# Another order of the stages on all four engines of a one-core transformer tower

## What is computed

```python
x = emb[tokens] * sqrt(D) + pe
scores = einsum('d,bijd->bij', attn_scale, tanh((x@Wq + bq)[:, :, None, :] + (x@Wk + bk)[:, None, :, :]))
h = layer_norm(x + softmax(scores) @ (x@Wv + bv) @ Wo + bo) ; h = layer_norm(h + relu(h@W1 + bf1)@W2 + bf2)
h = h + causal_attention_8_heads(ln(h))
t = ln(ln(h)) ; moe = the two best of 64 experts for every token ; shared = (silu(t@Ws1 + bs1)@Ws2 + bs2) * 0.25
out = h + ln(h) + (moe + shared) + silu(ln(moe + shared)@Wf1 + bf1)@Wf2 + bf2
```

## Time and profile before

| | us |
|---|---|
| median of three runs | 824.73 |
| the profiled execution | 828.12 |
| its span, first to last instruction | 826.1 |
| first `add` | 25.27 |
| end of the last `add` | 505.5 |
| count of all tokens (L1649) | 583.23 |

### The profile page before, as it was taken

The page is one execution under the profiler, slowest core; times in us unless marked ns, Lnnn a source line. Parts: engine busy times, 40 slices in busy tenths (PEclk is TensorE's granted clock), DMA queues, the critical chain, the costliest instruction groups (busy, mean ns, idle before and its releaser), DMA issues.

```text
span 826.1 us, 21375 instructions
## 1 busy us (share of the span) xinstructions
PE 742.8 (90%) x7238; PEld 600.6 (73%) x7238; DVE 622.6 (75%) x1635; ACT 623.8 (76%) x1471; POOL 353.2 (43%) x466
## 2 busy tenths in 40 slices
PE   0656799999999999999999999987789999999898
PEld 0533567777777677677677677765679999999787
DVE  0699999999999999999999996543423435443685
ACT  0477899999999999999999999764235556665354
POOL 3101223444644544554544543666126545555111
PEclk9988999999999999999999999998889999999999
DMA  3940000000000000000000000000299999994511
GB/s 82 261 93 6 7 2 7 14 13 12 18 14 11 16 16 12 16 16 11 16 16 12 11 16 7 16 15 25 88 342 393 376 394 401 320 359 160 160 32 38
DMA packets 50096, 78.99 MB, mean 96 GB/s; under 512 B 7428, under 2 KB 34203, under 8 KB 50000
## 3 DMA queue, kind: packets, MB, share of 16 engines
q1 hardware_dynamic: 33824, 65.01, 22.9%
q0 software_dynamic: 5664, 7.92, 3.5%
q10 hardware_dynamic: 10512, 4.83, 2.1%
HBM read 63.95 MB, written 15.92 MB: 97 GB/s over the span
## 4 chain that ended last, share of the span: by engine, by line
DVE 45%; PE 33%; issue 11%; POOL 3%; ACT 2%; SPq 2%; DMA 2%; ACTq 1%; POOLq 0%; DVEq 0%
DVE arena L939 27%; PE big L1693 9%; PE b_qk L1704 4%; PE b_s L1704 4%; DVE mx L1069 3%; PE big L1749 3%; SPq L404 2%; PE b_s L1762 2%; DVE stat_h L982 1%; PE b_qk L1762 1%; DVE stat_x L982 1%; POOL rows_dram L616 1%; PE big L1496 1%; PE b_s L1383 1%; PE b_t L1686 1%
## 5 line engine op out<-in xcount | busy, mean ns | idle before, releaser
L939 DVE TENSOR_TENSOR arena<-qT,b_qk 128x2304 f32<-128x2304 f32 x128 | 323.2, 2540 | 3.4 <-PE b_s L1383 3.2
L683 ACT ACTIVATE arena<-arena 128x2304 f32<-128x2304 f32 x128 | 272.4, 2133 | 10.3 <-DVE arena L939 10.2
L1383 PE MATMUL b_s<-arena,apad 128*32 128x192 f32 x3072 | 149.6, 333 | 4.2 <-ACT arena L683 3.5
L846 ACT ACTIVATE act_h<-big,arena 128x128 f32<-128x128 f32 x324 | 92.7, 369 | 71.9 <-PE big L1693 66.1
L1383 PEld LDWEIGHTS b_s<-arena,apad 128*32 128x32 f32 x3072 | 89.5, 111 | 48.3 <-issue 13.8
L651 POOL DMA_INDIRECT eo_dram<-gT,toff x81 | 79.8, 985 | 96.6 <-DVE gT L1268 92.9
L579 POOL TENSOR_TENSOR kept<-kept,rs 96x384 f32<-96x384 f32 x64 | 52.7, 824 | 120.7 <-DVE rs L1075 120.5
L1693 PE MATMUL big<-hbT,arena 128*128 128x128 f32 x648 | 87.2, 278 | 1.6 <-DVE hbT L1257 1.6
L747 ACT ACTIVATE kept<-big,mx 96x96 f32<-96x96 f32 x256 | 83.5, 350 | 2.6 <-DVE mx L1069 2.6
L1693 PEld LDWEIGHTS big<-hbT,arena 128*128 128x128 f32 x648 | 80.1, 194 | 2.0 <-issue 1.3
L616 POOL DMA_INDIRECT rows_dram<-rows_now,slots x64 | 61.4, 960 | 42.8 <-DVE slots L1123 30.2
(11 more groups left out here) (227 smaller groups left out, 1410.8 us busy)
## 6 DMA issues: line engine op xcount, KB each, us to landing
arena<-in_wpack SPq DMA_DIRECT2D x81, 578.0 KB, 10.0
prT<-rows_dram ACTq DMA_DIRECT2D x73, 64.5 KB
rows_dram<-act_h SPq DMA_DIRECT2D x1, 4128.0 KB, 23.4
arena<-eo_dram SPq DMA_DIRECT2D x4, 512.0 KB, 7.4
x_dram<-res SPq DMA_DIRECT2D x16, 96.0 KB, 1.7
out<-of SPq DMA_DIRECT2D x12, 128.0 KB, 1.8
eo_dram<-gT,toff POOLq DMA_INDIRECT x81, 5.6
rows_dram<-rows_now,slots POOLq DMA_INDIRECT x64, 2.3
```

The source lines that it names most:

```text
L683: act.activation(v, v, ACT.Tanh).then_inc(s["tanh"], 1)
L846: last = act.activation(act_h[:, i, c * TILE:(c + 1) * TILE], big[i][:, c * TILE:(c + 1) * TILE], ACT.Silu, bias=wslot[:, slot, 2 * DFF + ...
L939: dve.tensor_tensor(ring[c % TRING].rearrange("p (x m n) -> p x m n", m=CQ, n=N), qv.unsqueeze(3).to_broadcast([D, SPLIT * QG, CQ, N]), kv ...
L1383: last = pe.matmul(b_s[32 * a:32 * a + 32, 0:SPLIT * N], apad[:, 31 - line:63 - line], t[:, :, a, m, :], start=(line == 0), stop=(line == ...
```

## The change

No stage is added, removed or altered, and every stage runs as often as before. The four `body` lists and the three bank orders are written in another order, and each list also starts at another point of the pair (so many offsets k differ by one without a difference in time). TensorE's `setup` of the weights moves from n = -1 to n = 0, behind `xs_turn`, `qk` and two `score`s of pair 0; VectorE's `setup` moves behind five `add`s of pair 0; TensorE's `products` moves behind all eight `score`s of pair 0. GpSimd's `setup` (four small constants) moves from n = 0 to n = 2, ScalarE's `products` within n = 2.

The diff, cut to the lines that the prediction speaks of:

```diff
...
 YA_ORDER = [
-    (2, "attend1"), (1, "v_rows"), (5, "logits"), (5, "ranks"), (2, "ffn2"),
+    (5, "logits"), (1, "v_rows"), (5, "ranks"), (2, "ffn2"), (1, "attend1"),
 ]
...
             def body(n):
-                at(n, 4, normalise, 0)
                 at(n, 1, keep_x)
...
-                at(n, 0, setup)
+                at(n, 4, roots_h1)
+                at(n, 3, normalise, 1)
                 at(n, -1, gather_emb, 1)
+                at(n, 2, root, "x2")
...
-                at(n, 3, inv_sums, 1)
-                at(n, 2, x2_stats)
-                at(n, 4, h1_shift)
...
+                at(n, 1, x1_stats)
+                at(n, 0, setup)
+                at(n, 2, variance, "h0")
...
+                at(n, 1, x2_stats)
+                at(n, 3, h1_shift)
+                at(n, 2, inv_sums, 1)
...
-                at(n, 1, products)
-                at(n, 1, score, 0)
-                at(n, 4, heads_m, 0)
-                at(n, 1, score, 1)
-                at(n, -1, setup)
...
+                at(n, 1, score, 7)
+                at(n, 3, pr_turn, 0)
+                at_end(n, 6, shared2, 1)
+                at(n, 1, products)
...
+                at(n, 0, setup)
+                at(n, 0, score, 2)
...
```

More of the change, by code:

```diff
@@ L621, in body @@
             def body(n):
[L622 removed]
                 at(n, 1, keep_x)
[L624 to L625 removed]
+                at(n, 4, normalise, 2)
+                at(n, 2, setup)
+                at(n, 3, root, "h0")
                 at(n, 6, scatter_rows, 1)
[L627 to L630, removed]
                 at(n, 6, cum_pair)
                 at(n, 4, normalise, 3)
+                at(n, -1, gather_emb, 0)
+                at(n, 2, root, "x1")
                 at(n, 5, both_hot)
                 at(n, 5, counted)
[L635 removed]
+                at(n, 5, keep_rows)
+                at(n, 5, residual)
+                at(n, 3, normalise, 0)
+                at(n, 5, scatter_rows, 0)
+                at(n, 4, roots_h1)
+                at(n, 3, normalise, 1)
                 at(n, -1, gather_emb, 1)
[L637 to L640 removed]
+                at(n, 2, root, "x2")
             in_turns(body)
@@ L820, in body @@
                 at(n, 2, relu, 1)
+                at(n, 0, tanh, 1)
                 at(n, 1, exp1)
[L822 to L826, removed]
             act.wait_ge(s["ld_a"], 16 * 5)
@@ L1592, in body @@
             def body(n):
-                at_end(n, 5, shared1, 1)
-                at(n, 2, p1_turn)
-                at(n, 1, products)
-                at(n, 1, score, 0)
-                at(n, 4, heads_m, 0)
-                at(n, 1, score, 1)
-                at(n, -1, setup)
-                at_end(n, 6, shared2, 0)
-                at(n, 4, pr_turn, 1)
                 at(n, 4, scores, 3)
-                at(n, 4, o_begin)
-                at(n, 5, tn_turn)
-                at(n, 2, attend1)
-                at(n, 1, score, 2)
+                at(n, 5, logits)
                 at(n, 4, attend2, 0)
+                at(n, 1, score, 3)
+                at(n, 4, pr_turn, 2)
                 at(n, 4, heads_m, 1)
-                at(n, 4, pr_turn, 2)
-                at(n, 1, v_rows)
-                at(n, 1, score, 3)
-                at(n, 5, logits)
-                at_end(n, 6, shared2, 1)
-                at(n, 4, attend2, 1)
-                at_end(n, 5, shared1, 2)
-                at(n, 4, heads_m, 2)
                 at(n, 3, xa_turn)
                 at(n, 1, score, 4)
-                at(n, 4, pr_turn, 3)
+                at(n, 4, heads_m, 2)
+                at(n, 1, v_rows)
+                at(n, 0, xs_turn)
                 at(n, 3, heads_g, 0)
                 at(n, 3, heads_g, 1)
-                at(n, 5, ranks)
-                at(n, 0, xs_turn)
-                at(n, 4, heads_m, 3)
+                at(n, 1, score, 5)
+                at(n, 4, pr_turn, 3)
                 at(n, 3, scores, 0)
```

109 lines of the change are left out of this document (61 added, 48 removed), and 8 rows, old and new, of the table BIG_ORDER.

## The result

The changed kernel takes 802.42 us (median of 4 runs, 801.71 to 803.38). The kernel before, on the same chip, takes 824.69. The ratio is 0.9725, with a 95% interval of 0.9708 to 0.9742. The forecast was 801.6 us, so the sum was right; its terms were less so, as the parts show.

What follows compares the result with a forecast made beforehand. VectorE was taken as the bound once the pipeline has filled. Terms -12.4 + 0.8 - 2.5 - 1.0 - 6.0 - 2.0 = -23.1 bring the profiled 828.1 to 805.0; that execution stood 3.4 above the median, so 801.6 us, range 792 to 814.

Steps and rivals of the forecast that it cites:

- The start: At the kernel's start: `xs_turn` becomes TensorE's first stage, so the first `add` falls at 12.8 us, -12.4 us.
- The terms +0.8, -2.5 and -1.0: First pairs: VectorE's `setup` among `add`s +0.8 us, `products` behind pair 0's scores -2.5, shorter `qk` waits -1.0.
- `products` ... I take -2.5: Behind pair 0's last `score`: `products` takes 6.2 us, mostly covered by the ring of four `add`s; -2.5 us.
- The cover: Between pair 0's last `add` and pair 1's fifth: VectorE has some 12.6 us of waiting and work while `products` runs.
- VectorE's own time: Full part: `h1_shift` and `x_rows` no longer wait for POOL's `normalise`; 0.5 us a pair, -6.0 over 12 pairs.
- the choice of meetings: Full part, new VectorE meetings with POOL: `x1_norm` beside `both_hot` taken as 0, `x2_norm` beside `keep_x` as 0.2 us.
- The 30.9 us: Full part: expected period of a pair, with ScalarE at 30.5 us and TensorE not far off.
- Waits that move: Full part: `logits` and `xs_turn` cost TensorE up to 0.9 us, but nothing reaches VectorE; 0.
- The emptying: After the last `add`: `x2`'s root and `normalise` 2 come ahead of POOL's `scatter_rows` 1; -2.0 us, between +3 and -5.
- The second phase: After the count of all tokens: as long as before.
- Only the start pays: Rival: in the full part, waits or new POOL meetings take back VectorE's freed 0.9 us; 810.6 us, chance 0.20.
- TensorE starts at the low clock: Rival, at the start: low clock until `products`, the 2.5 us come back, `qk` waits grow; 805 us, chance 0.08.

Runs made afterwards that it cites:

- seventh experiment: The changed kernel with VectorE's `x1_norm` moved ahead of `one_hot`; ratio 0.9741 to the kernel before.
- fourth: The kernel before with only VectorE's `inv_sums` 1 moved behind `h1_shift` and `x_rows` ahead of `inv_sums` 2; ratio 0.9996 to the kernel before.
- eighth: The changed kernel with POOL's `scatter_rows` 0 moved behind `roots_h1` and `normalise` 1 in all passes; ratio 1.0275 to the kernel before.
- eleventh: The kernel before with `setup`, `products` and POOL's `setup` moved, `inv_sums` 1 behind `h1_shift`, `x_rows` ahead of `inv_sums` 2, POOL's `x2` root ahead of `scatter_rows` 1; ratio 0.9796.
- sixth experiment: The changed kernel with VectorE's `inv_sums` 1 put back ahead of `x2_stats` and `h1_shift`; ratio 0.9797 to the kernel before.
- ninth experiment: The changed kernel with POOL's `scatter_rows` 0 behind `roots_h1` and `normalise` 1 only in the last passes, where no new pair starts; ratio 0.9801 to the kernel before.

## Why the prediction was right, and where it was not

*The start.* Right: -12.7 for -12.4. What the prediction gave as one chain, though, is three gates in a row (folds, `products`, POOL's `setup`), each of which holds back everything while it stands. The third was not in it: moved stages were followed on TensorE and VectorE, and POOL's `setup` got no price.

*The filling of the pipeline.* The terms +0.8, -2.5 and -1.0 give -2.7; it was -4.8. The fifth `add`'s wait went wholly (-3.25), the folds cost 0.66, `qk`'s waits fell by 1.7, a new wait of `xa_norm` for POOL's root took 0.9, and the shorter `h1_shift` and `x_rows` of pairs in this stretch gave about 1.3. The step "`products` ... I take -2.5" was undersized: it took 4.0 us, not 6.2. Its loads were there at its first matmul in both kernels; but the first 24 matmuls, which follow each other without a gap in both, took 2.94 us where they had taken 5.32 right behind TensorE's wait of 6.29 us. The cover, on the other side, is 1.8 + 0.42 + 9.95 = 12.2 us by its rows and not 12.6.

*VectorE's own time.* The mechanism was right, the size too small: -0.67 a pair for -0.5, -7.5 us in all from pair 5 on for -6.0. By rows, `h1_shift` and `x_rows` give 0.476 + 0.414 = 0.89; `x1_norm` takes back 0.16 and `xa_norm` 0.08, which leaves 0.65. The step that failed is the choice of meetings: `x1_norm` was taken as 0 ("so it shows no sign of a doubled rate"), and came, the long `x1_norm` that the prediction names as a sign of being wrong; `x2_norm` was taken as 0.2, and did not come. The rule that speaks against the order was named and then set aside on a duration. The Trainium skill ("VectorE: DVE Perf Modes", section "Mode 2×_2P — use both read ports for one tensor") has a mode in which an instruction with one source in SBUF uses both read ports, and "SBUF — State Buffer", section "SBUF: two separate sides", has such an instruction wait for GpSimd. The trace agrees that it waits (0.504 against 0.340, and 0.340 again once `both_hot` comes later); its duration without a meeting, the same as that of a two-input instruction, did not tell. The 30.9 us also allowed for ScalarE as the next bound, and nothing of that was needed: the seventh experiment, with `x1_norm` out of the way, runs at 30.54.

*Waits that move.* "Nothing here reaches VectorE" held: it waits nowhere in the full part, and `logits` costs TensorE 0.3 us a pair. The fourth and eighth experiments show how near the edge was: `h1_shift` and `x_rows` are shorter in both, but with POOL's root behind a scatter the time does not change in the one and the period is 34.2 in the other.

*The emptying.* Wrong in sign: -2.0 for +2.6. The step that failed took POOL's late root of `x2` as the limit of a round and put the moves of VectorE's lines at nothing there. In the old order the moves of `inv_sums` 1 and `x_rows` alone make the stretch 3.5 us longer (fourth experiment, 81.3 us), since `normalise` 1 then waits; in the eleventh it is 81.1 us with TensorE busy 65.6, as before. In the changed kernel it is not that move: with `inv_sums` 1 put back in the sixth experiment the stretch is still 80.2 us. There TensorE is busy 4.3 us longer, partly with more work and partly at the lower clock. Moving POOL's scatter there brought nothing or cost 6 us, and brought no root forward. What sets the 80.3 us is not shown by any run.

*The second phase.* Taken as unchanged, it is 2.8 us shorter. Half of it lies between the count and the first expert: 15.14 us at a granted clock of 0.81 before, 13.7 at 1.00 after. Over the profiles of all runs, whose second phase is the same, the stretch takes 239.8 to 242.9 us, so the difference need not be the change.

*The rivals.* "Only the start pays" falls with the period of 30.71. "TensorE starts at the low clock" did not come in the profiled execution: at 22.82 a `score` took 1.18, and `products` ran short. In the profiles of the eighth and ninth experiments, in the same order up to pair 5, the granted clock was 0.50 ahead of `products`, and it went with 1.5 us, not the 3.4 of the rival. Errors of +4.6 and -2.8 at the end and of -3.9 ahead of it largely cancel, so the nearness of 801.6 to 802.4 is partly luck.

## What to carry to other kernels

An early start is worth nothing until every gate behind it is moved: follow each moved stage on all engines, to the first buffer that is full and the first queue that waits for a late load. Time saved on a full engine shows only if the small results that it waits for, here a root on a half idle engine, are ordered to come earlier as well. A move that is free while the pipeline is full can still cost where it empties: look there at what the moved line now stands behind. When instructions are moved, list what the engine that shares SBUF with it does at each new place, and give a meeting a price until a row excludes it.

## What was not expected of the hardware

In the ninth experiment an idle stretch of 2.5 us on TensorE was followed by some 10 us at a granted clock of 0.50 (498 to 514 us, in the rows above) with TensorE busy without a gap from 500.42 on, and by an emptying 7.7 us longer; after, without the idle stretch, had 1.00 there. Two executions in the same order, after and the ninth experiment up to pair 5, had their low stretches at different times, and 1.5 us between them. VectorE's instruction with one SBUF source and 128 columns is stretched by POOL work (`x1_norm` beside `both_hot`, 0.504 against 0.340), and one of the two `xa_norm` took 0.443 against 0.337 beside the issue of an indirect DMA, while the 128 `add`s with one source in PSUM took 2.518 to 2.556 us wherever POOL stood.
